# Folding the Hadamard product: one butterfly level moved to VectorE, token normalisation and rounding to ScalarE, and every engine's work put in a new order

## The reference, cut to what matters

```
x = x + layernorm(attention(layernorm(x)))        # 16 heads of 32, causal, score - distance, Wq Wk Wv Wo, biases
x = x + layernorm(ffn(layernorm(x)))

def ffn(x, weight):
    xh = x @ H                                     # H: Hadamard 512x512, [[h, h], [h, -h]] / sqrt(512)
    scale = max(|xh| over the row, 1e-5) / 7
    xq = clip(round(xh / scale), -8, 7) * scale    # 4 bits
    return xq @ ternary(weight).T                  # -1, 0, 1 times one scale for each row of weight
```

## Time and profile before

| | |
|---|---|
| median of three runs | 1359.95 us |
| profiled execution, its own time | 1356.21 us |
| its span, first to last instruction | 1354.7 us |
| granted TensorE clock, mean | 0.984 of 2.4 GHz |
| PE busy | 1261.2 us, 93% |
| DVE / ACT / POOL busy | 960.7 / 629.5 / 565.4 us (71 / 46 / 42%) |
| DMA engines, mean busy share | 36% between 95 and 1272 us |

### The profile page before, as it was taken

How to read it: one execution, slowest core, us unless ns; L and a number is a source line. 1 busy time by engine, 2 the same in 40 slices (tenths; PEclk the granted TensorE clock), 3 DMA queues, 4 the chain that set the end, 5 groups by cost and what they waited for, 6 DMA issues and landing times.

```text
span 1354.7 us, 45217 instructions
## 1 busy us (share of the span) xinstructions
PE 1261.2 (93%) x19136; PEld 810.4 (60%) x19136; DVE 960.7 (71%) x2424; ACT 629.5 (46%) x1395; POOL 565.4 (42%) x714
## 2 busy tenths in 40 slices
PE   3789999999999999999999999999999999999862
PEld 2556666666656666656666666566666566666430
DVE  3766777677767677777777778776776877766673
ACT  2344454445444444544444454444454444444431
POOL 0133444343444444345444344444434454443341
PEclk9899999999999999999999999999999999999896
DMA  7433443234344333334433233343333344322310
GB/s 250 100 77 93 112 111 95 74 86 112 81 110 111 95 80 90 101 81 111 111 98 89 76 104 108 82 111 95 91 89 92 83 108 111 104 70 64 82 47 17
DMA packets 69773, 128.87 MB, mean 95 GB/s; under 512 B 14880, under 2 KB 15648, under 8 KB 69472
## 3 DMA queue, kind: packets, MB, share of 16 engines
q1 hardware_dynamic: 64880, 108.90, 31.6%
q0 software_dynamic: 4688, 17.04, 3.4%
HBM read 41.49 MB, written 16.78 MB: 43 GB/s over the span
## 4 chain that ended last, share of the span: by engine, by line
PE 88%; DVE 4%; issue 3%; SPq 2%; DMA 2%; POOL 1%; ACT 1%; POOLq 0%; DVEq 0%; ACTq 0%
PE f_job L1006 47%; PE f_job L1163 8%; PE f_o L1130 5%; PE f_st L1110 5%; PE f_o L1135 5%; PE f_job L1181 4%; PE f_job L1090 3%; PE f_job L1035 3%; PE f_job L1154 3%; PE f_job L1078 2%; SPq L315 2%; PE f_job L1171 1%; DMA f_stacks<-f_stage 1%; PE f_job L1066 1%; POOL f_z L403 1%
## 5 line engine op out<-in xcount | busy, mean ns | idle before, releaser
L382 POOL TENSOR_SCALAR_AFFINE_SELECT f_PT<-f_PT 64x512 f32<-64x512 f32 (+1 forms) x256 | 170.9, 687 | 169.2 <-ACT f_PT L502 119.3
L397 POOL TENSOR_TENSOR f_square<-f_stage 128x512 bf16<-128x512 f16 x128 | 131.7, 1049 | 228.5 <-ACT f_stage L480 228.5
L388 POOL TENSOR_TENSOR f_OTl<-f_o,f_OTh 128x256 f16<-128x256 f32 x128 | 85.8, 670 | 261.2 <-ACT f_OTh L520 261.2
L480 ACT ACTIVATE f_stage<-f_job,f_bias 128x256 f16<-128x256 f32 x256 | 106.6, 467 | 134.8 <-PE f_job L1006 134.7
L730 DVE SCALAR_TENSOR_TENSOR f_stage<-f_job,f_bias,f_stage 128x256 f16<-128x256 f32 x256 | 111.3, 478 | 76.9 <-ACT f_stage L480 76.7
L502 ACT ACTIVATE f_PT<-f_st 128x512 f32<-128x512 f32 x192 | 108.8, 595 | 115.8 <-PE f_st L1110 115.8
L1006 PE MATMUL f_job<-f_xTh,f_wqh 128*128 128x256 f16 x512 | 140.6, 275 | 9.3 <-DVE f_wkl L628 5.9
L1006 PE MATMUL f_job<-f_xTh,f_wkl 128*128 128x256 f16 x512 | 140.1, 274 | 0.0
L1006 PE MATMUL f_job<-f_xTh,f_wkh 128*128 128x256 f16 x512 | 140.1, 274 | 0.0
L1006 PE MATMUL f_job<-f_xTl,f_wkh 128*128 128x256 f16 x512 | 140.1, 274 | 0.0
L1006 PE MATMUL f_job<-f_xTl,f_wqh 128*128 128x256 f16 x512 | 140.1, 274 | 0.0
(11 more groups left out here) (155 smaller groups left out, 3023.0 us busy)
## 6 DMA issues: line engine op xcount, KB each, us to landing
f_stacks<-f_stage SPq DMA_DIRECT2D x384, 128.0 KB
f_xin<-x SPq DMA_DIRECT2D x32, 512.0 KB, 4.5
f_xres<-x SPq DMA_DIRECT2D x32, 512.0 KB, 3.8
out<-f_z POOLq DMA_DIRECT2D x32, 512.0 KB, 4.2
f_Vmix<-f_V SPq DMA_DIRECT2D x32, 256.0 KB, 3.3
f_Vmix<-f_V SPq DMA_DIRECT2D x64, 128.0 KB, 3.3
f_stacks<-rows_const SPq DMA_DIRECT2D x3, 512.0 KB, 4.7
f_stacks<-wqT SPq DMA_DIRECT2D x1, 1024.0 KB, 8.1
```

The lines of the kernel that those rows point to most:

```text
L382: nc.gpsimd.affine_select(out=d, in_=d, compare_op=ALU.is_ge, fill=0.0, base=odd * SUB, pattern=[[0, 4], [0, TP], [1, SUB]], channel_multi ...
L388: nc.gpsimd.tensor_tensor(OT[s % 2][1][:, g, :], o32[:, g % 2, :], OT[s % 2][0][:, g, :], ALU.subtract).then_inc(OTl_made, 1)
L397: nc.gpsimd.tensor_tensor(square[:, 2 * m + pair, :], h, h, ALU.mult).then_inc(squared, 1)
L480: nc.scalar.activation(stage[:, 2 * m, g, :], bank("qk", g)[:, m * W2:(m + 1) * W2], ACT.Identity, bias=bias[:, m, g:g + 1]).then_inc(qk_h ...
```

## The change

Since H = [[h, h], [h, -h]] with h of 256x256, x @ H is [(left + right) @ h, (left - right) @ h] for the halves of a row. The changed kernel does sum and difference on DVE (`fold`, four instructions of 128x256 a step, written to `y`), transposes those, and multiplies with h: 8 matmuls a tile still, but of 256 columns. `front_norm` and `level` move from DVE to ACT (the first with an offset column made by the new `front_offset`; the second without the `min`). In `normalise` the scaled heads stay in PSUM rather than in `o32`, and `weigh` waits for the last instruction of `normalise` instead of its second. The fallback bound on the variance of x1 is 2^12 instead of 2^14. The loops of PE, DVE, ACT and POOL and the table `ORDER` are rearranged; SP's program is as it was.

```diff
-MEAN, VARIANCE = 1.0, (2.0 ** -2, 2.0 ** 14)
+MEAN, VARIANCE = 1.0, (2.0 ** -2, 2.0 ** 12)
...
-        had = sb("had", [P, KC, D], F16)
+        had = sb("had", [P, TP, W2], F16)
...
@@ program of ScalarE @@
+            def front_norm(m, t):
+                act.wait_ge(f_off_made, m + 1)
+                nc.scalar.activation(xin[m % 2][:, t, :], xin[m % 2][:, t, :], ACT.Identity, bias=f_off[:, t:t + 1],
+                                     scale=f_rstd[:, t:t + 1]).then_inc(xn_made, 1)
...
@@ program of ScalarE @@
+            def level(k, t):
+                act.wait_ge(rounded, TP * k + t + 1)
+                until(act, q_turned, TP * (k - 1) + t + 1)
+                nc.scalar.activation(q16[:, t, :], y[:, t, :], ACT.Identity, bias=unround_col[:]).then_inc(q_made, 1)
...
@@ program of VectorE @@
-            def front_norm(m):
+            def front_offset(m):
                 dve.wait_ge(f_rstd_made, m + 1)
-                for t in range(TP):
-                    nc.vector.tensor_scalar(xin[m % 2][:, t, :], xin[m % 2][:, t, :], f_mv[:, t, 0:1],
-                                            f_rstd[:, t:t + 1], ALU.subtract, ALU.mult).then_inc(xn_made, 1)
+                nc.vector.scalar_tensor_tensor(f_off, f_mv[:, :, 0], -1.0, f_rstd, ALU.mult, ALU.mult)\
+                  .then_inc(f_off_made, 1)
...
-                nc.vector.tensor_tensor(o32[:, g % 2, :], ps_o[g % 2][:, 0:W2], inverse[:, g % 2, :],
-                                        ALU.mult).then_inc(o_scaled, 1)
+                heads = ps_o[g % 2][:, 0:W2]
+                nc.vector.tensor_tensor(heads, heads, inverse[:, g % 2, :], ALU.mult).then_inc(o_scaled, 1)
...
-                nc.vector.scalar_tensor_tensor(o32[:, g % 2, :], inverse[:, g % 2, :], 2.0, o32[:, g % 2, :],
+                nc.vector.scalar_tensor_tensor(o32[:, g % 2, :], inverse[:, g % 2, :], 2.0, heads,
                                                ALU.subtract, ALU.mult).then_inc(o32_made, 1)
...
@@ program of VectorE @@
+            def fold(k, t):
+                dve.wait_ge(x1_made, TP * k + t + 1)
+                left, right = x1[k % 2][:, t, 0:W2], x1[k % 2][:, t, W2:D]
+                nc.vector.tensor_tensor(y[:, t, 0:W2], left, right, ALU.add).then_inc(folded, 1)
+                nc.vector.tensor_tensor(y[:, t, W2:D], left, right, ALU.subtract).then_inc(folded, 1)
...
@@ program of VectorE @@
-            def level(k, t):
-                dve.wait_ge(rounded, TP * k + t + 1)
-                nc.vector.tensor_scalar(q16[:, t, :], y[:, t, :], ROUND, QMAX, ALU.subtract,
-                                        ALU.min).then_inc(q_made, 1)
...
             def transform(k, t):
-                for h in range(2):
-                    for c in range(KC):
-                        mm = pe.matmul(bank("h", t)[:], x2T[h][:, c, t * P:(t + 1) * P], had[:, c, :],
-                                       start=(h == 0 and c == 0), stop=(h == 1 and c == KC - 1))
+                for half in range(2):
+                    dst = bank("h", t)[:, half * W2:(half + 1) * W2]
+                    for h in range(2):
+                        for c in range(2):
+                            mm = pe.matmul(dst, x2T[h][:, 2 * half + c, t * P:(t + 1) * P], had[:, c, :],
+                                           start=(h == 0 and c == 0), stop=(h == 1 and c == 1))
```

More of the change, by code:

```diff
@@ L559, in _ @@
                     qk_high_part(n, 0)
+                if has(k - 1):
+                    level(k - 1, 1)
                 if s == -1:
@@ L616, in _ @@
                     heads_high(s, 2)
+                if has(k):
+                    level(k, 0)
+                if s == -1:
+                    keep_tern()
                 if has(k):
@@ L864, in _ @@
             front_stats(0)
-            front_norm(0)
+            front_offset(0)
             front_low(0, 0)
@@ L872, in _ @@
                 n, m, k = s + 1, s + 2, s - 1
-                if has(k - 1):
-                    level(k - 1, 1)
                 if has(m):
                     front_stats(m)
+                if has(n):
+                    qk_low_part(n, 0)
+                if has(m):
+                    front_offset(m)
+                if has(n):
+                    qk_low_part(n, 1)
+                if has(k):
+                    normalise(k, 3)
                 if s == 0:
                     weight_guards()
+                if has(n):
+                    qk_low_part(n, 2)
+                if has(k - 1):
+                    scale_out(k - 1, 0)
                 if s == -1:
@@ L901, in _ @@
                 if has(k):
-                    y_out(k, 0)
                     y_out(k, 1)
@@ L908, in _ @@
                     residual(k)
+                    fold(k, 0)
+                    fold(k, 1)
                 if has(s):
@@ L1200, in _ @@
                     qk(n, 2)
+                if has(k - 1):
+                    second(k - 1, 0)
+                if has(n):
+                    qk(n, 3)
                 if has(s):
@@ L1203, in _ @@
                     keys(s, 0, 1)
-                if has(n):
-                    qk(n, 3)
+                if has(m):
+                    front_tile(m, 0)
                 if has(k - 1):
-                    second(k - 1, 0)
                     second(k - 1, 1)
-                if has(k):
-                    out_product(k, 0)
+                if has(m):
+                    front_tile(m, 1)
                 if has(s):
@@ L1213, in _ @@
                     keys(s, 1, 1)
+                if has(k):
+                    out_product(k, 0)
+                    out_product(k, 1)
+                if has(s):
                     weigh(s, 0)
-                if has(k):
-                    out_product(k, 1)
+                    keys(s, 2, 0)
+                    keys(s, 2, 1)
                 if has(n):
@@ L1237, in _ @@
                     keys(s, 3, 1)
+                if has(n):
+                    values(n, 1)
+                if has(k):
+                    turn_x2(k, 0)
+                if s == -1:
+                    turn_tern()
+                if has(k):
+                    turn_x2(k, 1)
+                if has(n):
+                    scores(n, 2)
+                if has(s):
                     weigh(s, 2)
                 if has(n):
-                    scores(n, 2)
                     scores(n, 3)
-                if has(m):
-                    front_tile(m, 0)
                 if has(k):
@@ L1247, in _ @@
                     weigh(s, 3)
-                if has(m):
-                    front_tile(m, 1)
                 if has(k):
```

178 lines of the change are left out of this document (82 added, 96 removed).

## The result

The changed kernel takes 1298.93 us (median of four runs, 1295.19 to 1300.94); the kernel before took 1361.51 beside it (median of four, 1359.37 to 1363.44). The ratio is 0.9538, with a 95% interval of 0.9509 to 0.9566.

A forecast was written before the change was run, and what follows sets the result against it. PE's own work was taken to set the time. From 1356.2 us, -51.6 for the transform, +3 for PE's waits, +1.6 head and -1.0 tail gave 1308.2, or 1312 for the median; range 1302 to 1330.

The forecast's parts named there:

- The transform: PE's product with H: a tile goes from 1.73 to 0.87 us, saving 0.86, or 51.6 us over 60 tiles.
- The sign named for it: Evidence that would show the forecast right: the transform's new matmuls on PE at 109 to 114 ns each.
- PE's new pass (38.39 - 1.73 = 36.66): PE's gapless pass of 38.39 us less 1.73 for the transforms, giving 36.66 us, no other matmul added or removed.
- VectorE at the boundary: Loop over the pass boundary: VectorE and ScalarE need 5.72 us against PE's 5.86, fitting with 0.1 to 0.2 to spare.
- Contention with POOL: Folds beside POOL's third clear_future: VectorE charged 0.4 to 0.8 us a pass, PE waiting 3 us in all, bounds 0 and 15.
- Rival (4): Slower than before: VectorE's two-SBUF instructions stand still for all POOL work beside them; 1379 us at 3.2 a pass, chance 0.04.
- The head: Start of the run, with weight guards behind two of four q/k low halves: +1.6 us, bounds -1 and +5.
- The tail: Last two passes: transforms -2.6 us, folds +1.4, level on ScalarE +0.4; together -1.0, bounds -4 and +3.
- The sum: Whole run: 1356.2 - 51.6 + 3 + 1.6 - 1.0 = 1308.2 us, 1312 for the median.
- more is gained: The outcome of a time below 1303 us, given a chance of 0.02.

The follow-up runs named there:

- e1: Kernel before with only the butterfly (folds, turns of y, matmuls of 256 columns), all orders as before; 1351.22 us, ratio 0.9915 to the kernel before.
- e2: Changed kernel with the whole Hadamard matrix again: no folds, x1 turned directly, 512 columns, new order kept; 1326.18 us, ratio 0.974 to the kernel before.
- e6: e2 with the second turn of x2 moved behind scores 2; 1333.13 us, ratio 0.9785 to the kernel before.
- e5: Changed kernel with two small column instructions of z_stats issued at the end of the pass before; 1277.76 us, ratio 0.9375 to the kernel before.
- e3: Changed kernel with one weight guard in each of steps 1, 2, 3 and 5, not all in s = 0; 1295.52 us, ratio 0.9502.
- e8: Changed kernel with the edits of e5 and e3, plus finish_out ahead of y_root in the last two steps; 1270.57 us, ratio 0.9316.

## Why the prediction was wrong, point by point

**The transform: right.** 0.85 us a tile measured, 0.86 forecast. The sign named for it, 109 to 114 ns a matmul, is met in the old place (0.88 / 8 = 110 in e1) and not in the new one (0.98 / 8 = 122), where both products cost 0.1 more.

**PE's new pass (38.39 - 1.73 = 36.66): this is the step that failed.** A pass in which PE waited for nobody took 36.11 us. The step took the other groups of matmuls at the length that they had in the old order, and carried the old pauses into the new average. The new order changes the first without a change of work: -0.30 for the turns of x2, -0.15 for the second front tile, +0.2 for the two transforms behind scores 3 and `weigh` 3, and some 0.3 in smaller seams that I did not separate; with the old product the pass is 37.82. The second: 14.3 us of pauses without an engine behind them in the passes before (10.0 of them in the earlier trace rows), 0.5 in e2. Together with 2 us of waits that went, these make about 33 of the order's 35 us. e6 shows one seam by itself (6 us); the others are read from the chain and were not tried singly.

**VectorE at the boundary: it fits, as forecast.** In e5, PE waits neither at qk 1 nor at `turn_q` between 135 and 1160 us. `level` took 712 ns where a pitch of 0.65 was assumed, `front_norm` 811, and ScalarE's 21.76 us in the pass meet the 22 forecast. VectorE's own load was 30.25 (29 forecast).

**Contention with POOL: the right mechanism, with the wrong instructions.** The charge was 0.4 to 0.8 us a pass on the folds, and PE's wait 0.1 (0.5 at most). VectorE lost 1.4 us a pass on two column instructions, which the sum held at nothing, and 0.6 on the folds; PE lost 0.52 us a pass (e5), 15.4 us where 3 were forecast. It stood at `turn_x2`, not at the boundary. Rival (4) had VectorE standing still for the whole of POOL's work. The column instructions come near that, the folds don't (1.4 us lost beside 2.3); of the 2.0 us that VectorE lost, PE lost a quarter, and I read the rest as slack in the order. The Trainium skill, "VectorE: DVE Perf Modes", section "Two Vector instructions with no wait between them", has the second SBUF operand go through an interface shared with GpSimd. These rows agree, and show that a small instruction is no safer: the two of 128x2 lost 0.9 and 0.5 us in the mean, a fold beside POOL's work 0.46.

**The head: +6.0, not +1.6.** The four guards behind two low halves cost 7.7 us against a head without them (e3). What they cost in their old place wasn't run, so how much of the miss belongs to the move (forecast 3.7) and how much to the gains set against it (-1.2, -1.7, -1.9) stays open.

**The tail: +2.9, not -1.0.** The last transforms gave 5.14 - 3.58 = 1.6, not 2.6. `finish_out` on POOL ran beside the last residual, which took 3.40 us instead of 1.41 (VectorE and POOL below). Setting it ahead of `y_root` in e8 made the tail only 0.7 shorter, so part of the miss stays open.

```profile
1253.43 3.40 DVE L825 SCALAR_TENSOR_TENSOR f_x<-f_y,f_small,f_xres 128x512 f32<-128x512 f32 x2 [0.81 <-POOL f_small L374]
```

```profile
1253.37 2.92 POOL L407 TENSOR_TENSOR f_z<-f_z,f_x 128x512 f32<-128x512 f32 x2
```

**The sum.** -48.6 for the passes should have been -51.3 for the butterfly, -35 for the order and +15.4 for VectorE's lateness: -71, measured -70.1. The two misses have opposite signs, so the total is nearer to the forecast than its parts are; that is luck. The range was too narrow because "more is gained" had 0.02: the working had priced the order's losses one by one and given its gains on PE no bounds at all.

## What to carry to other kernels

When all engines are reordered, price PE's groups by what will stand ahead of each (short matmuls ahead were dear here), and give the gain of new seams bounds as well as the losses. Before a tiny VectorE instruction with two SBUF operands is costed at nothing, look at what POOL does at that moment: beside selects it lasted about as long as one or two of them, and moving it to another place in the pass was worth 1.5% of this kernel. A delay on an engine with slack can push its later work into the next conflict, so remove the first one and measure again before treating the second.

## What the hardware showed that was not expected

- A 128x2 instruction with two SBUF operands took 1045 ns in the mean beside POOL's select and 161 ns away from it; the select itself wasn't lengthened by it (0.63 us each in the four of 708.36). `normalise`'s last instruction, with its heads in PSUM, kept 421 ns.
- Four float32 transposes take 0.58 to 0.59 us behind short matmuls (keys, `weigh`, scores) and 0.43 to 0.44 behind long products or four of their own; eight products of 512 columns take 1.73 us behind float32 transposes and 1.83 behind short matmuls, eight of 256 columns 0.88 and 0.98. In the order of this change such seams are worth about half a microsecond a pass.
- PE's pauses with no engine behind them recur mostly at 630 and 1762 matmuls in the old order, last 0.2 to 1.6 us, and all 43 in three traces end 2.2 to 2.9 us after the start of a 16 KB packet of the instruction queue q8. Adding 64 short instructions moved them to other passes and made the kernel 0.5% faster (0.9934 to 0.9967).
